# No fill of an unused tile between the GpSimd queue's indirect transfers

## What is computed

```python
gates = jax.nn.softmax(xt @ gate_w, axis=-1)
top_v, top_i = jax.lax.top_k(gates, K)            # K = 2 of E = 8
top_v = top_v / jnp.sum(top_v, axis=-1, keepdims=True)
h = jnp.einsum('nd,edf->enf', xt, fc_w)           # f = 512
h = jax.nn.gelu(h, approximate=False)
eo = jnp.einsum('enf,efd->end', h, proj_w)
```

## Time and profile before

| | us |
|---|---|
| median of 3 runs | 679.75 |
| the profiled execution | 682.17 |
| its span in the profile | 680.3 |
| layer 0's slots, first transpose to last down product | 113.6 to 206.8 |
| layer 1's slots | 551.0 to 668.7 |
| TensorE busy | 576.5 (85% of the span) |
| POOL busy | 207.7 (31%) |

### The profile page before, as it was taken

The page is one execution under the profiler, slowest core; times in us unless marked ns, Lnnn a source line. Parts: engine busy times, 40 slices in busy tenths (PEclk is TensorE's granted clock), DMA queues, the critical chain, the costliest instruction groups (busy, mean ns, idle before and its releaser), DMA issues.

```text
span 680.3 us, 12175 instructions
## 1 busy us (share of the span) xinstructions
PE 576.5 (85%) x3853; PEld 478.4 (70%) x3854; DVE 437.6 (64%) x1576; ACT 233.0 (34%) x515; POOL 207.7 (31%) x258
## 2 busy tenths in 40 slices
PE   5799817879997999999998679989996369999993
PEld 2477703769995568888987557746776159899993
DVE  8878883214365665566687686787778837555573
ACT  2355201235553423444433033325541013333331
POOL 6100057744557024920000000000000778733332
PEclk9899657979996999989989888989995579989997
DMA  9999922212254000000000350021000122211243
GB/s 220 184 185 248 267 75 63 67 52 72 71 151 141 0 2 1 1 1 1 1 0 1 119 129 1 1 82 44 1 1 0 52 59 62 62 47 47 56 123 112
DMA packets 61016, 47.67 MB, mean 70 GB/s; under 512 B 6266, under 2 KB 54819, under 8 KB 60806
## 3 DMA queue, kind: packets, MB, share of 16 engines
q1 hardware_dynamic: 56422, 37.68, 24.2%
q0 software_dynamic: 4544, 9.38, 4.1%
HBM read 27.53 MB, written 19.51 MB: 69 GB/s over the span
## 4 chain that ended last, share of the span: by engine, by line
PE 53%; issue 20%; SPq 12%; DVE 10%; another core or an unknown queue 2%; ACT 1%; DMA 1%; DVEq 0%; POOL 0%; POOLq 0%; ACTq 0%
PE bank L2186 16%; PE bank L2197 9%; PE bank L1826 7%; SPq L420 7%; PE bank L2008 5%; SPq L409 2%; SPq L414 2%; PE bank L1815 2%; PE bank L1816 2%; PE bank L1817 2%; PE bank L2174 2%; DVE X L1397 1%; DVE XW L991 1%; PE bank L1851 1%
## 5 line engine op out<-in xcount | busy, mean ns | idle before, releaser
L590 POOL DMA_INDIRECT xw<-XW,slot_i x64 | 62.4, 975 | 317.6 <-DVE slot_i L1149 296.7
L2186 PE MATMUL bank<-xT,wcur 128*128 128x128 f32 x936 | 124.5, 285 | 11.3 <-ACT xT L762 11.3
L2186 PEld LDWEIGHTS bank<-xT,wcur 128*128 128x128 f32 x936 | 117.3, 201 | 12.7 <-ACT xT L762 10.7
L606 POOL DMA_INDIRECT yt<-Y,dest_i x78 | 75.9, 973 | 90.0 <-ACT Y L775 44.6
L1257 DVE COPY wcur<-WA 128x512 f32 x78 | 37.8, 485 | 54.3 <-PE bank L2186 51.4
L1397 DVE SCALAR_TENSOR_TENSOR X<-bank,G,X 128x128 f32<-128x128 f32 x128 | 36.0, 344 | 47.4 <-PE bank L1826 38.7
L842 ACT ACTIVATE hT<-bank,b_cols 128x512 f32<-128x512 f32 x64 | 43.5, 687 | 65.7 <-PE bank L1817 65.2
L1826 PE MATMUL bank<-WC,hT 128*128 128x128 f32 x512 | 65.4, 283 | 0.0
L1826 PEld LDWEIGHTS bank<-WC,hT 128*128 128x128 f32 x512 | 62.6, 198 | 2.8 <-ACT hT L842 0.9
L1272 DVE TENSOR_TENSOR hT<-gb,bank 128x512 f32<-128x512 f32 x39 | 26.8, 688 | 44.5 <-ACT gb L767 38.6
L767 ACT ACTIVATE gb<-bank 128x512 f32<-128x512 f32 x39 | 23.3, 597 | 57.3 <-PE bank L2186 46.7
(11 more groups left out here) (390 smaller groups left out, 1142.4 us busy)
## 6 DMA issues: line engine op xcount, KB each, us to landing
xw<-pad_rows SPq DMA_DIRECT2D x34, 260.0 KB, 9.2
xrow<-xw SPq DMA_DIRECT2D x78, 65.0 KB
WA<-in_fc_dram SPq DMA_DIRECT2D x16, 256.0 KB, 6.5
YT<-yt SPq DMA_DIRECT2D x16, 256.0 KB, 2.9
WA<-in_pj_dram SPq DMA_DIRECT2D x8, 256.0 KB, 5.5
WB<-in_fc_dram SPq DMA_DIRECT2D x8, 256.0 KB, 4.6
WB<-in_pj_dram SPq DMA_DIRECT2D x8, 256.0 KB, 6.1
yt<-Y,dest_i POOLq DMA_INDIRECT x78
```

The costliest lines, as they stand in the source:

```text
L590: pool.indirect_dma_start(out=xw_dram, out_offset=bass.IndirectOffsetOnAxis(ap=slot_i[:, choice, tile:tile + 1], axis=0), in_=XW[:, tile, ...
L606: pool.indirect_dma_start(out=yt_dram, out_offset=bass.IndirectOffsetOnAxis(ap=dest_i[:, t:t + 1], axis=0), in_=Y[:, s, :], in_offset=None ...
L2186: ins = pe.matmul(dst, wcur[:, s4, at:at + P], xT[s4 % 2][:, :], start=True, stop=True)
```

## The change

`pause` and its three uses are taken out. POOL's queue holds the same transfers in the same order with the same waits, and nothing between them.

```diff
-            def pause(layer, layers):
-
-                if layer in layers:
-                    link(pool.memset(M[:, 1, :], 0.0))
-
             def experts(layer):
...
                 for tile in range(GT, GT + GT // 2):
                     for choice in range(TOPK):
                         scatter(layer, 1, tile, choice)
-                        pause(layer, (0, 1))
                 for t in range(SLOTS):
                     put(layer, t)
                     if t < GT // 2:
                         for choice in range(TOPK):
-                            pause(layer, (1,))
                             scatter(layer, 2, GT + GT // 2 + t, choice)
-                        pause(layer, (1,))
```

## The result

The changed kernel takes 692.87 us (median of 4 runs, 691.85 to 694.65), beside 680.32 us for the kernel before (679.54 to 682.32). The ratio is 1.0177, with a 95% interval of 1.0157 to 1.0198: 12.5 us slower. The forecast was 5.7 us slower, with a range that ended at 691.0. The profiled execution took 694.65 us, its span is 692.8, that is 12.5 us over the span of before.

What follows compares the result with a forecast made beforehand. It took TensorE as busy for 85% of the span, POOL's own time as worth nothing, and dense POOL transfers as delaying signals. 0 + 0 + 1.5 + 4.0 + 4.0 - 3.8 = +5.7 us, median 685.5; range 675.5 to 691 us.

Steps and rivals of the forecast that it cites:

- (a): POOL's saved time by itself, 4.1 us in layer 0 and 10.2 in layer 1, off the chain: 0 us.
- (b): DVE's weight copies get faster without memsets beside them, 0.47 us per slot: taken as 0 us, bounds 0 to 4.2 gained.
- (c): Start of each layer, beside group 1's eight unpaced transfers: first transpose's signal comes x later, 4.0 us, bounds 0 to 4.7.
- x: Added lateness of the first transpose's signal in each layer: 4.0 us, bounds 0 to 4.7.
- (d): Layer 0's run with puts: starts x later, ends 2.5 us - x earlier; layer x - 2.5 = +1.5 us, bounds -2.5 to +2.2.
- hold: An instruction starts long after what it waits for was done, beside POOL transfers without memsets; seen: 2.15, 4.0, 8.5 us.
- (e): Layer 1's run with puts 0 to 3 and group 2, now unpaced: a new hold, +4.0 us, bounds 0 to 7.2.
- (f): Layer 1, slot 12: the existing hold goes as POOL has caught up, -3.8 us, bounds -3.8 to 0.
- the second: Rival: full holds everywhere, 4.7 us at both starts and 7.2 in (e): +10.3, 690 us; chance 0.17.
- The fourth: Rival: holds cancel or are bound to fixed program places, not POOL: within 1.4 us of 679.75; chance 0.08.
- The third: Rival: holds come from backlog, not density; known holds shrink, no new ones: -6.3, 673.5 us; chance 0.16.

Runs made afterwards that it cites:

- e17: The changed kernel again, on a fifth chip where the kernel before takes 663.90 us: 663.55 us, ratio 0.9989.
- e7: Kernel before without the memsets of group 1 in both layers, the twelve of layer 1's group 2 kept: 690.95 us beside 682.09, ratio 1.0129.
- e9: Kernel before with all 28 memsets still linked but clearing one column each, transfers 1.35 us apart: 692.98 us beside 681.89, ratio 1.0159.
- e8: Kernel before without memsets; in group 1 POOL waits for each transfer's landing, layer 1's group 2 is unpaced: 694.34 us beside 682.09, ratio 1.0171.
- e11: Kernel before with twelve memsets added in layer 0's group 2, as layer 1's has: 681.78 us beside 681.89, ratio 0.9993.
- e12: Kernel before with group 1 waiting for each landing in place of memsets, group 2 of both layers with twelve memsets: 688.16 us beside 681.89, ratio 1.0095.
- e10: Kernel before with each of the 28 pauses made two memsets in a row: 694.68 us beside 681.89, ratio 1.0173.
- e14: Kernel before with memsets after every transfer of groups 1 and 2 in both layers and after puts 4 to 23: 662.33 us beside 663.91, ratio 0.9975.
- e16: Kernel before with a memset added after each of puts 4 to 23 of both layers: 658.51 us beside 663.91, ratio 0.9917.
- e1: Kernel before without the twelve memsets of layer 1's group 2, group 1's sixteen kept: 664.58 us beside 663.98, ratio 1.0006.
- e13: The same kernel as e1 again, on a fourth chip: 664.23 us beside 663.91 for the kernel before, ratio 1.0004.

## Why the prediction was right and wrong

The direction was right, and the mechanism too where signals are late at all. The size was less than half of what was measured, and the range ended 1.9 us too low. By its steps:

- **(a), POOL's own time: right.** 16 us less work on POOL bring nothing where signals come in time, and nothing else changes there (e17, 0.9989).
- **(b), DVE's weight copies: right, 0.** Those of `WA` went from a mean of 485 to 434 ns over the whole kernel, as they should without memsets beside them, and the time grew. The Trainium skill (SBUF — State Buffer, Who interferes with whom) has DVE's two-port copies and GpSimd exclude each other, and the trace agrees as far as the copies go. It also says that PE and ACT never wait on anyone there. That is said of SBUF's ports; here ACT stood 9.1 us and PE's matmuls were spread out beside POOL's transfers, so the rule says nothing of this case's effect.
- **(c), the first late signal of each layer: the step that failed.** The text said that it can't last longer than POOL's unpaced run, so x was at most 4.7 us, and took 4.0. Measured from the first transpose, it is 6.9 us in layer 0 and 6.8 in layer 1, outside the bound in both. The bound took two wrong things together. It took the signal to come at the latest when POOL's last transfer is issued, where it comes 2.0 to 2.2 us after that. And it took the signal to come anywhere within such a run, where in all eight starts with transfers 1.26 or 1.35 us apart, in the jobs with late signals, it came behind the run. The trace of before already spoke against the first. The prediction read only slot 7's transpose there, which was copied 0.6 us before the end of POOL's last transfer at 140.81. The up product of slot 6, right behind it, was done at 131.55 + 1.06 = 132.61, and ACT started on it at 143.07, 10.5 us late and 2.3 us after that transfer's end:

```profile
131.55 1.06 PE L2186 MATMUL bank<-xT,wcur 128*128 128x128 f32 x8
...
143.07 0.60 ACT L767 ACTIVATE hT<-bank 128x512 f32<-128x512 f32 x1 [2.57 <-PE bank L2186]
```

- **(d), layer 0's run with puts: the sum nearly right, the picture not.** The forecast for the whole layer was x - 2.5 = +1.5. The layer gave back 6.9 - 3.9 = 3.0 us instead of 2.5, and with x = 6.9 the step's own formula gives +4.4; measured are +3.9. But the run was not the 14.8 us of 12 transfers with one hold that ends with it. POOL stopped after nine transfers, at 142.18, for a late `Y`, issued the last three from 144.98 on, and ended at 148.50; and one late signal was read in the middle of it:

```profile
139.66 0.60 ACT L759 ACTIVATE hT<-bank 128x512 f32<-128x512 f32 x1 [3.84 <-remote]
...
144.98 0.99 POOL L606 DMA_INDIRECT yt<-Y,dest_i  x1 [2.81 <-ACT Y L767]
```

- **(e) and (f), layer 1's run with puts and slot 12: right.** Forecast +4.0 - 3.8 = +0.2, measured 8.7 - 6.8 = +1.9. Slot 12's loss is gone: PE's steps are 2.79 us from 598.72 on. So (e) is 1.9 + 3.8 = 5.7 us, inside its bounds of 0 to 7.2. e7, in which this run keeps its pauses, is 1.7 us below the changed kernel in its job, which agrees but is within the spread of the runs. What stood in (e)'s place was not one hold: ACT's waits of 2 to 5 us and PE's own matmuls starting late make up the 5.7 us together.

With x = 6.9 and 6.8 for 4.0 twice the forecast's own sum is 4.4 + 6.8 + 4.0 - 3.8 = 11.4 us: the one bound of (c) carries 5.7 of the 6.8 us that the forecast missed. Of the rivals the second, full holds everywhere (+10.3), was the nearest; its number is so near partly by luck, since its 4.7 us for each start were too low and its 7.2 us for (e) too high. The fourth, that late signals are bound to the program's own places and not to POOL, falls by e9 and e8, in which they move with POOL's spacing. The third, that the backlog counts and not the density, is half true: behind a slower group 1 the backlog is worked off in a longer dense run, and the lateness moves there (e8, e11, e12). The density is still the condition, since the starts get clean with spacing alone.

What the prediction had no case for is that the effect can be absent altogether. Its reasoning holds in three of six jobs. In the other three taking memsets out costs nothing, and in the one of them that ran the changed kernel it takes as long as the kernel before. That the job of the first comparison was of the first kind is luck as far as the prediction goes.

**Open.** What differs between the jobs isn't shown, and whether it is the chip isn't either. Besides the late signals one thing differs, in every trace: how many increments of semaphores it holds. Of the 512 increments with which group 0's transfers land, all 512 are in each trace of the 664 us jobs and 138 to 159 in each of the others, though group 0 has no memset in any kernel. Group 1's are 256; in the jobs with late signals the changed kernel's trace holds 40 of them, that of before 96, e10's 212, and e8's and e12's, where POOL waits for each landing, 255 and 256. So in the same jobs, and the more the denser the transfers, increments either come several at once or are not recorded; the traces don't tell which. Every execution on record carries a span and a granted clock, so each was recorded in some form, and that the recording itself holds up signals and instructions in those jobs is a rival that no run here tests. Whether a kernel without any unpaced stretch (e14, e16) is free of late signals on a chip that has them was not answered, since both jobs with it had none in any kernel. And the path on which PE's signals and PE's own instructions meet POOL's transfers isn't seen in any row.

## What to carry to other kernels

Before a wait that the profile can't assign is costed, look for a dense run of GpSimd's indirect transfers beside it. Don't take the end of that run as the latest time of the signal: behind a run of eight it came 1.9 to 2.7 us after the last transfer was issued, though in longer runs some signals came within. Spacing such transfers takes the lateness away where they are spaced and gives it back where the queue catches up, so place the dense stretch where no other engine has a signal that matters. And compare variants in the same job, and in more than one, on more than one chip: a difference of 1.8% in one was none in another.

## What the runs showed of the hardware that was not expected

- The same program takes 680 to 682 us in three jobs and 664 us in three others, on other chips as far as these are on record. 16 to 17 us of that are late signals in two loops: 87.6 and 110.3 us against 75.3 and 105.5, or 76.6 and 105.4, for the nearest kernel there (e1, e13).
- While GpSimd issues indirect transfers 1.26 us apart, PE's signal of a finished transpose reached ACT 9.1 to 9.9 us late, at 1.78 us apart 2.2 to 4.2, at 2.36 it was 1.0 and 1.2, and from 2.5 on 0.04. In the 664 us jobs it was 0.04 at every spacing. Late signals behind a dense run came 0.6 to 2.7 us after its last transfer was issued (2.2 and 2.0 in the changed kernel, 2.55 in e8, 1.85 in e11, 0.6 in e12); in longer runs some were read within it (at 139.66 in the changed kernel).
- In the jobs with late signals a trace holds 138 to 159 of the 512 increments with which group 0's transfers land, in the others all 512.
- In such a stretch PE starts matmuls that wait for nothing 0.7 us apart or at multiples of that, where 0.11 us is its step in the same product elsewhere.
